# Four probability buffers, and the probability products of eight units issued together

## The chip, the core and the metric

The kernel runs on one core of a Trainium2 chip. The metric is the device time of one execution in microseconds (us). A core has five engines with queues of their own: TensorE (PE in the profile; PEld is its weight load), VectorE (DVE), ScalarE (ACT), GpSimd (POOL) and SyncE (SP, which issues the DMAs). They are ordered among each other only by semaphores.

## The reference

There are 8 batch rows of 512 tokens and 256 features. Each goes through a cross-attention with 16 heads of size 16 and then through a two-layer network without a nonlinearity, both with a normalisation ahead and a residual behind:

```python
qh = split_heads(layernorm(x) @ Wq.T + bq) / sqrt(16)
kh = split_heads(ctx @ Wk.T + bk)
vh = split_heads(ctx @ Wv.T + bv)
attn = softmax(einsum('bhqd,bhkd->bhqk', qh, kh), axis=-1)     # 512 x 512 for each head
y = x + einsum('bhqk,bhkd->bhqd', attn, vh) @ Wo.T + bo
h1 = layernorm(y) @ W1[b].T + b1[b]                            # 256 -> 1024, weights of its own for each b
out = y + h1 @ W2[b].T + b2[b]                                 # 1024 -> 256
```

## The kernel before

One batch row is one turn of a loop: `turns` writes out turns 0, 1, 6 and 7 and runs turns 2 to 5 as a hardware loop. A turn has 64 units, numbered u. The 16 heads form four quads of four heads. A unit is one head of a quad and one block of 128 keys, and four units that follow each other (a group, kc or n in the code, 16 groups in a turn) are the four heads of a quad for the same key block.

For each unit TensorE computes two score products:

- `st` (L449) gives the scores transposed, keys on the partitions, into one of two PSUM banks (`st0`, `st1`). ScalarE takes their exponential into a probability buffer (`exp`, L728).
- `nat` (L439) gives the scores of a unit 28 units ahead the other way round into one of three banks. VectorE takes their row maximum (L896), which is later subtracted inside `st`.

`st` and `nat` use 64 and 63 rows of the PE array, in the two halves of it, so that a `st` and a `nat` run side by side. `st(u)` waits until `exp(u-2)` has emptied its bank.

When the four exponentials of a group are there, `pv` (L463) multiplies the four heads' probabilities with their values. These four products use 32 columns of the array each and also run side by side. The trace shows eight matmul records for each `pv`: a first pass of four and a second pass of four. One `pv` fills one bank, `pv_bank`, over the four key blocks of a quad. ScalarE copies the sums out after groups 3 and 11 (`even_quad`, L756) and 7 and 15 (`odd_quad`, L768).

The order of TensorE's work is written out by hand. `turn` takes two units at a time (u0 = 0, 2, 4, ...): two `st` with their `nat`, at every second pair a `pv`, then the `jobs` of these two units. Jobs are all the rest, spread over the 64 units by tables: the values, keys and queries of the next row, the output projection of the previous row, its network (`w21_part`, L549, multiplies the two weight matrices together; `z` applies the product), transposes (L481), and the transpose of a quad's maxima (`maxT`, L495). Jobs have waits of their own. The one that matters below is at u = 39: the second half of the transposed `yT` overwrites bank `misc1`, and waits until ScalarE has copied the weight product out of it (`w21_copy_first`, L784, which stands behind `exp(38)` in ScalarE's order).

ScalarE too has a fixed order: the exponentials by unit, and between them by the unit's number its other work. After `exp(6)` and after `exp(7)` come two activations each that normalise the next row (L773). After `exp(22)` come the copy of the last quarter of the projections (L748) and the masking of the even quad's result (L761).

Probabilities have two buffers, `probs0` and `probs1`, group n in buffer n mod 2. `exp` of a group's first unit waits until the `pv` of two groups ago is done. `pv(n)` is issued after the `st` of units 4n+6 and 4n+7, four units behind the group's last: at u0 = 6, 10, 14, ..., 62 and at u0 = 2 of the next turn.

Of the kernel before, what the change touches and what calls it, by code (L numbers as in the profile page):

```python
# [30 lines left out]
ACT = mybir.ActivationFunctionType  # L31
AX = mybir.AxisListType

P = 128
B = 8
S = 512
# [8 lines left out]
UNITS = QUADS * 16  # L45
# [33 lines left out]
def xattn_ffn(nc, x, ctxT, wqT, bq, wkT, bk, wvT, bv, woT, bo, w1, b1, w2T, b2, out):  # L79
    with ExitStack() as stack:  # L80
        def sb(name, shape, dt=F32):
            return stack.enter_context(nc.sbuf_tensor(name, shape, dt))
# [4 lines left out]
        def sem(name):  # L87
            return stack.enter_context(nc.semaphore(name))
# [32 lines left out]
        vs = sb("vs", [P, C, H, 32])  # L121
        neg_max = sb("neg_max", [P, 2, 16])
        max_hi = sb("max_hi", [16, P], F32R)
        probs = [sb(f"probs{i}", [P, 4, S]) for i in range(2)]
        even_ctx = sb("even_ctx", [P, S])
        even_sum = sb("even_sum", [P, S])
        pair_ctx = sb("pair_ctx", [P, S])
# [48 lines left out]
        pv_done = sem("pv_done")  # L176
# [9 lines left out]
        exp_done = sem("exp_done")  # L186
# [59 lines left out]
        def st_of(u, prep):  # L246

            return (st_bank + nat_bank)[u % 3] if not prep and u >= LAST_ST else st_bank[u % 2]

        def nats_of(b, u, post, prep):  # L250

            if not post and FIRST_LEAD + 2 * u < u + LEAD:
                return [(b, FIRST_LEAD + 2 * u + i) for i in range(2)]
            n = u + LEAD
            if n < UNITS:
                return [(b, n)]
            return [(b + 1, n - UNITS)] if prep else []
# [4 lines left out]
        def wait(eng, s, value):  # L262

            if not (isinstance(value, int) and value <= 0):
                eng.wait_ge(s, value)
# [158 lines left out]
        def _(pe):  # L424
# [7 lines left out]
            def nat(b, n):  # L432
                g, c, (jj, jp) = n // 16, n % 16 // 4, NAT_HEADS[n % 4]
                rows = slice(HALF * jp, HALF * jp + KN)
                if n % 16 == 0:
                    wait(pe, stacked[g], STACKS * (b + 1))

                wait(pe, max_done, UNITS * b + {0: -3, 1: 0, 2: -1, UNITS - 1: n - 1}.get(n, n - 2))
                mm(nat_of(n)[:, :], qs[rows, 2 * g + jj, c * P:(c + 1) * P], ks[rows, 2 * g + jj, :],  # L439
                   start=True, stop=True).then_inc(nat_done, 1)  # L440

            def st(b, u, prep):
                g, kc, (jj, jp) = u // 16, u % 16 // 4, ST_HEADS[u % 4]
                rows = slice(HALF * jp, HALF * jp + KS)
                if u % 16 == 0:
                    wait(pe, max_rows, 16 * (4 * b + g + 1))

                wait(pe, exp_done, UNITS * b + u - (2 if not prep and u >= LAST_ST + 2 else 1))
                mm(st_of(u, prep)[:, :], ks[rows, 2 * g + jj, kc * P:(kc + 1) * P], qs[rows, 2 * g + jj, :],  # L449
                   start=True, stop=True).then_inc(st_done, 1)  # L450

            def pv(b, n):
                g, kc = n // 4, n % 4
                if kc == 0:
                    wait(pe, v_stacked, 4 * b + g + 1)
                    pair = 2 * b + g // 2
                    if g % 2:
                        wait(pe, even_out, pair + 1)
                    else:
                        wait(pe, odd_out, pair)  # L460
                wait(pe, exp_done, UNITS * b + 4 * n + 4)
                for j in range(4):
                    last = mm(pv_bank[32 * j:32 * j + 32, :], vs[:, kc, 4 * g + j, :],  # L463
                              probs[n % 2][:, j, :], start=(kc == 0), stop=(kc == 3),
                              tile_position=(0, 32 * j), skip_group_check=True)
                last.then_inc(pv_done, 1)

# [167 lines left out]
            def turn(b, post, prep, load):  # L635
                for u0 in range(0, UNITS, 2):
                    for u in (u0, u0 + 1):
                        st(b, u, prep)
                        for row, n in nats_of(b, u, post, prep):
                            nat(row, n)  # L640
                    if u0 % 4 == 2:
                        if u0 > 4:
                            pv(b, u0 // 4 - 1)
                        elif post:
                            pv(b - 1, 15)
                    for u in (u0, u0 + 1):
                        jobs(b, u, post, prep)

# [28 lines left out]
            pe.wait_ge(rows_set, 2)  # L677
            pe.wait_ge(ones_in, 16)
            turns(pe, turn)
            pv(LAST, 15)  # L680
            pe.wait_ge(last_comb, 1)
            pe.wait_ge(exp_done, UNITS * B)
# [39 lines left out]
        def _(act):  # L722
            def exp(b, u, prep):
                kc, j = u // 4, u % 4
                wait(act, st_done, UNITS * b + u + 1)
                if j == 0:
                    wait(act, pv_done, 16 * b + kc - 1)
                act.activation(probs[kc % 2][:, j, :], st_of(u, prep)[:, :], ACT.Exp).then_inc(exp_done, 1)  # L728

            def xT_copy(b, f, bank):  # L730
                wait(act, xT_done, 2 * b + f + 1)
# [73 lines left out]
            def turn(b, post, prep, load):  # L805
                for u in range(UNITS):
                    exp(b, u, prep)
                    if post:
                        if u == 0:
# [468 lines left out]
```

## Time and profile before

| | |
|---|---|
| device time, median of 3 runs | 616.38 us (615.13 to 617.4) |
| span of the profiled execution, first to last instruction | 613.0 us |
| TensorE busy | 584.0 us (95%) |
| VectorE busy | 458.9 us (75%) |
| ScalarE busy | 397.0 us (65%) |
| GpSimd busy | 221.2 us (36%) |
| mean granted TensorE clock | 0.989 |
| starts of turns 0 to 7, first `st` | 42.4, 106.9, 176.9, 247.5, 318.2, 388.9, 459.6, 529.5 us |

The profiled execution's own device time is not given apart from its span; the span is 3.4 us below the median of the runs. The turns in the middle are alike: each takes 70.7 us. The last turn takes 60 us up to its last products, because it prepares no next row. Matmuls are pipelined, so a record's duration is longer than the distance to the next start. How long TensorE is held by something is read here from the distance between starts.

### The profile page before, as it was taken

The page shows a single profiled execution, that of the slowest core. Times are in us where ns is not written, and L with a number is a line of the kernel's source. Part 1 is how long each engine was busy: PE and PEld are TensorE (multiplying, and loading weights), DVE is VectorE, ACT ScalarE, POOL GpSimd, SP SyncE. Part 2 cuts the span into 40 slices and gives each one's busy share as a digit, 9 for nine tenths or more (in the row PEclk, how much of TensorE's full clock was granted, in tenths as well). Part 3 has the DMA queues.
Part 4 walks back from the last instruction along what each step waited for, and adds up shares of the span by engine and source line. Part 5 has one row for each costly group of instructions (what it writes and reads, how often), then busy time and mean ns, then how long its engine had stood idle before and what let it go on. Part 6 is the DMA issues. An engine that isn't in the chain of part 4 may idle for free.

```text
span 613.0 us, 11485 instructions
## 1 busy us (share of the span) xinstructions
PE 584.0 (95%) x3380; PEld 296.0 (48%) x3380; DVE 458.9 (75%) x854; ACT 397.0 (65%) x746; POOL 221.2 (36%) x298
## 2 busy tenths in 40 slices
PE   7899989999999999999999999999999999889997
PEld 7545323545454544545444544445445454335457
DVE  5698787878888778787888777878788788786124
ACT  4217776776767586776667776676767766776741
POOL 5011028213660148212570138411481146313721
PEclk9969999999999999999999999999999999999999
DMA  8730333263224614254132823256042622260100
GB/s 291 186 93 2 86 90 105 54 215 115 81 62 131 213 40 140 54 194 133 45 95 55 264 61 117 47 161 189 8 137 53 208 54 76 66 208 2 69 21 34
DMA packets 34076, 65.23 MB, mean 106 GB/s; under 512 B 9778, under 2 KB 11642, under 8 KB 31994
## 3 DMA queue, kind: packets, MB, share of 16 engines
q1 hardware_dynamic: 34042, 64.81, 35.6%
q8 instruction: 17, 0.28, 0.2%
q14 instruction: 17, 0.14, 0.1%
HBM read 34.65 MB, written 4.44 MB: 64 GB/s over the span
## 4 chain that ended last, share of the span: by engine, by line
PE 83%; ACT 7%; issue 3%; POOL 2%; DVE 2%; DMA 1%; SPq 1%; ACTq 0%; DVEq 0%; POOLq 0%
PE st L449 20%; PE misc L471 20%; PE pv L463 18%; PE misc L549 11%; PE nat L439 8%; ACT probs L728 4%; PE misc L481 2%; ACT hi L748 1%; PE nat L430 1%; DMA bq_in<-bq 1%; PE misc L530 1%; ACT normedT_hi L741 1%; PE nat L471 1%; ACT normedT_hi L734 0%; POOL b_part L1185 0%
## 5 line engine op out<-in xcount | busy, mean ns | idle before, releaser
L896 DVE TENSOR_REDUCE neg_max<-nat 128x1 f32<-128x512 f32 x512 | 330.5, 679 | 78.9 <-PE nat L439 77.9
L728 ACT ACTIVATE probs<-st 128x512 f32<-128x512 f32 x505 | 283.3, 597 | 161.8 <-PE st L449 156.9
L449 PE MATMUL st<-qs,ks 64*128 64x512 f32 x505 | 200.9, 461 | 18.7 <-ACT probs L728 18.6
L439 PE MATMUL nat<-ks,qs 63*128 63x512 f32 x512 | 208.1, 471 | 1.9 <-DMA qs<-hi 1.1
L463 PE MATMUL pv<-probs,vs 128*32 128x512 f32 x1024 | 136.4, 605 | 0.0
L449 PEld LDWEIGHTS st<-qs,ks 64*128 64x128 f32 x505 | 80.5, 185 | 112.0 <-ACT probs L728 73.6
L439 PEld LDWEIGHTS nat<-ks,qs 63*128 63x128 f32 x512 | 83.4, 187 | 11.8 <-DVE neg_max L896 7.0
L549 PE MATMUL misc<-w_in 128*128 128x256 f32 x256 | 80.7, 411 | 0.0
L1147 POOL TENSOR_TENSOR pair_ctx<-pair_ctx,inv_sum 128x512 f32<-128x512 f32 x15 | 19.1, 1276 | 118.7 <-DMA inv_sum<-inv_dram 118.7
L549 PEld LDWEIGHTS misc<-w_in 128*128 128x128 f32 x256 | 40.6, 189 | 42.9 <-issue 35.5
L463 PEld LDWEIGHTS pv<-probs,vs 128*32 128x32 f32 x1024 | 20.1, 108 | 38.7 <-issue 35.8
L1123 POOL TENSOR_SCALAR var_eps<-mean_var 128x4 f32<-128x4 f32 x16 | 3.6, 226 | 97.3 <-DVE mean_var L913 96.8
L918 DVE SCALAR_TENSOR_TENSOR lo<-misc,bqk,hi 128x512 fp32r<-128x512 f32 x30 | 22.5, 751 | 14.9 <-ACT hi L748 14.9
L1139 POOL COPY vs<-v_nat 128x256 f32<-128x256 f32 x32 | 12.6, 398 | 56.5 <-PE pv L463 44.2
L1157 POOL TENSOR_TENSOR ctx_lo<-ctx_in,ctx_hi 128x1024 fp32r<-128x1024 f32 x7 | 16.7, 2381 | 44.8 <-ACT ctx_hi L797 44.8
L1152 POOL TENSOR_TENSOR attnT_lo<-pair_ctx,attnT_hi 128x512 fp32r<-128x512 f32 x15 | 19.1, 1275 | 32.8 <-ACT attnT_hi L803 32.8
L1170 POOL TENSOR_TENSOR y<-y,b_all 128x256 f32<-128x256 f32 x28 | 19.6, 732 | 19.9 <-ACT normed L773 19.9
L962 DVE SCALAR_TENSOR_TENSOR pair_ctx<-pv,half_hi,even_ctx 128x512 f32<-128x512 f32 x15 | 11.3, 751 | 18.6 <-ACT odd_sum L768 18.6
L1185 POOL TENSOR_TENSOR b_part<-b_part 128x256 f32<-128x256 f32 x32 | 23.4, 732 | 2.5
L1163 POOL TENSOR_TENSOR y<-y,bo_all 128x256 f32<-128x256 f32 x32 | 22.6, 736 | 0.0
L924 DVE TENSOR_TENSOR normedT_lo<-misc,normedT_hi 128x512 fp32r<-128x512 f32 x28 | 19.0, 680 | 3.7 <-ACT normedT_hi L741 3.7
L748 ACT ACTIVATE hi<-misc,bqk 128x512 fp32r<-128x512 f32 x30 | 20.5, 684 | 1.2 <-PE misc L471 1.0
(168 smaller groups left out, 803.5 us busy)
## 6 DMA issues: line engine op xcount, KB each, us to landing
w_in<-w SPq DMA_DIRECT2D x8, 1024.0 KB
w_in<-w2T SPq DMA_DIRECT2D x8, 1024.0 KB
ks<-hi SPq DMA_DIRECT2D x64, 128.0 KB, 2.4
qs<-hi SPq DMA_DIRECT2D x64, 128.0 KB, 2.5
x_in<-x SPq DMA_DIRECT2D x8, 512.0 KB, 3.4
ctx_in<-ctxT SPq DMA_DIRECT2D x8, 512.0 KB, 4.3
ks<-lo SPq DMA_DIRECT2D x32, 128.0 KB, 2.4
qs<-lo SPq DMA_DIRECT2D x32, 128.0 KB, 2.6
```

What stands on the lines that cost most here:

```text
L439: mm(nat_of(n)[:, :], qs[rows, 2 * g + jj, c * P:(c + 1) * P], ks[rows, 2 * g + jj, :], start=True, stop=True).then_inc(nat_done, 1)
L449: mm(st_of(u, prep)[:, :], ks[rows, 2 * g + jj, kc * P:(kc + 1) * P], qs[rows, 2 * g + jj, :], start=True, stop=True).then_inc(st_done, 1)
L463: last = mm(pv_bank[32 * j:32 * j + 32, :], vs[:, kc, 4 * g + j, :], probs[n % 2][:, j, :], start=(kc == 0), stop=(kc == 3), tile_position ...
L471: last = mm(dst, left[i], right[j], start=start and n == 0, stop=stop and n == 2)
L549: last = mm(misc[bank][:, 0:D], w1_in[:, o, f * P:(f + 1) * P], w2_in[:, o, :], start=(o == 0), stop=(o == OC - 1))
L728: act.activation(probs[kc % 2][:, j, :], st_of(u, prep)[:, :], ACT.Exp).then_inc(exp_done, 1)
L748: act.activation(hi[:, which, m, :], misc[bank][:, :], ACT.Identity, bias=bqk[:, which, m:m + 1]).then_inc(hi_ready, 1)
L896: dve.tensor_reduce(neg_max[:, g % 2, at:at + 1], nat_of(n)[:, :], AX.X, ALU.max, negate=True).then_inc(max_done, 1)
L918: dve.scalar_tensor_tensor(lo[:, which, m, :], misc[bank][:, :], bqk[:, which, m:m + 1], hi[:, which, m, :].bitcast(F32), ALU.add, ALU.sub ...
L1163: last = pool.tensor_tensor(y[:, c, :], y[:, c, :], bo_all[:, :], ALU.add)
L1170: last = pool.tensor_tensor(y[:, c, :], y[:, c, :], b2_all[:, :], ALU.add)
L1185: pool.tensor_tensor(b2_part[:, k, :], b2_part[:, k, :], b2_part[:, 4, :], ALU.add).then_inc(b2_step, 1)
```

## The change

Four probability buffers replace two. Group n is in buffer n mod 4, and the first `exp` of a group waits for the `pv` of four groups ago. On TensorE two `pv` are issued together at every fourth pair of units: at u0 = 10 groups 0 and 1, at 18 groups 2 and 3, and so on up to 58; at u0 = 2 of the next turn groups 14 and 15. The last turn issues group 14 alone at u0 = 62 and group 15 at the end, as before. So the groups with odd numbers stay where they were and those with even numbers come four units later. Nothing is computed otherwise.

```diff
-        probs = [sb(f"probs{i}", [P, 4, S]) for i in range(2)]
+        probs = [sb(f"probs{i}", [P, 4, S]) for i in range(4)]
...
                 wait(pe, exp_done, UNITS * b + 4 * n + 4)
                 for j in range(4):
                     last = mm(pv_bank[32 * j:32 * j + 32, :], vs[:, kc, 4 * g + j, :],
-                              probs[n % 2][:, j, :], start=(kc == 0), stop=(kc == 3),
+                              probs[n % 4][:, j, :], start=(kc == 0), stop=(kc == 3),
                               tile_position=(0, 32 * j), skip_group_check=True)
...
-                    if u0 % 4 == 2:
-                        if u0 > 4:
-                            pv(b, u0 // 4 - 1)
-                        elif post:
-                            pv(b - 1, 15)
+                    if u0 % 8 == 2:
+                        for kc in (0, 1):
+                            if u0 > 8:
+                                pv(b, u0 // 4 - 2 + kc)
+                            elif post:
+                                pv(b - 1, 14 + kc)
+                    if u0 == UNITS - 2 and not prep:
+                        pv(b, 14)
...
                 if j == 0:
-                    wait(act, pv_done, 16 * b + kc - 1)
-                act.activation(probs[kc % 2][:, j, :], st_of(u, prep)[:, :], ACT.Exp).then_inc(exp_done, 1)
+                    wait(act, pv_done, 16 * b + kc - 3)
+                act.activation(probs[kc % 4][:, j, :], st_of(u, prep)[:, :], ACT.Exp).then_inc(exp_done, 1)
```

TensorE's order in a turn, from the `st` of unit 7 to the first job behind unit 11, before (L471 are projections of the next row, `x4` four products side by side):

```order
L449 MATMUL st1<-qs,ks 128x512
L439 MATMUL nat2<-ks,qs 128x512
L463 MATMUL pv<-probs0,vs 32x512 x4
L495 MATMUL misc1<-ident,neg_max 16x128
L449 MATMUL st0<-qs,ks 128x512
...
L471 MATMUL misc0<-ctx_lo,w_hi 128x512
L449 MATMUL st0<-qs,ks 128x512
...
L439 MATMUL nat0<-ks,qs 128x512
L463 MATMUL pv<-probs1,vs 32x512 x4
L481 MATMUL misc1<-ident,normed 128x128 x4
```

The same place in the changed kernel:

```order
L449 MATMUL st1<-qs,ks 128x512
L439 MATMUL nat2<-ks,qs 128x512
L495 MATMUL misc1<-ident,neg_max 16x128
L449 MATMUL st0<-qs,ks 128x512
...
L471 MATMUL misc0<-ctx_lo,w_hi 128x512
L449 MATMUL st0<-qs,ks 128x512
...
L439 MATMUL nat0<-ks,qs 128x512
L463 MATMUL pv<-probs0,vs 32x512 x4
L463 MATMUL pv<-probs1,vs 32x512 x4
L481 MATMUL misc1<-ident,normed 128x128 x4
```

The product of `probs0` has left its place between the units 7 and 8 and stands ahead of that of `probs1`, behind unit 11.

TensorE's order around units 38 and 39 in turn 1, before (the L481 in `misc1` is the second `yT`):

```order
L449 MATMUL st1<-qs,ks 128x512
L439 MATMUL nat0<-ks,qs 128x512
L463 MATMUL pv<-probs0,vs 32x512 x4
L481 MATMUL misc1<-ident,normed 128x128 x4
L449 MATMUL st0<-qs,ks 128x512
```

And in the changed kernel:

```order
L449 MATMUL st1<-qs,ks 128x512
L439 MATMUL nat0<-ks,qs 128x512
L481 MATMUL misc1<-ident,normed 128x128 x4
L449 MATMUL st0<-qs,ks 128x512
L439 MATMUL nat1<-ks,qs 128x512
```

The transpose into `misc1` now follows the score products of unit 39 directly. On the other engines no instruction changes its place; only the buffers and the value that the first `exp` of a group waits for are others.

## Rows read from the trace of the kernel before

**Rows 1.** The page, busy time of TensorE; the costliest group of ScalarE.

```profile
PE 584.0 (95%) x3380; PEld 296.0 (48%) x3380; DVE 458.9 (75%) x854; ACT 397.0 (65%) x746; POOL 221.2 (36%) x298
...
L728 ACT ACTIVATE probs<-st 128x512 f32<-128x512 f32 x505 | 283.3, 597 | 161.8 <-PE st L449 156.9
```

**Rows 2.** Busy time by engine in stretches: turn 3 and turn 7.

```profile
247.50:318.20 70.70, 69.07 (x407) 34.28 (x406) 55.77 (x104) 49.30 (x93) 27.84 (x38) 1.00 0.38 113
...
529.50:589.80 60.30, 55.88 (x322) 24.41 (x322) 31.39 (x59) 43.71 (x84) 21.80 (x29) 1.00 0.23 76
```

**Rows 3.** Waits of TensorE: who for whom, us in total, times, longest.

```profile
PE st L449 <- ACT probs L728: 18.6, 46, 0.6
```

**Rows 4.** Timeline (start, duration, engine, line, work, idle before): one `pv`, its second pass.

```profile
308.66 1.06 PE L463 MATMUL pv<-probs,vs 128*32 128x512 f32 x8
...
309.12 0.61 PE L463 MATMUL pv<-probs,vs 128*32 128x512 f32 x4
...
309.66 0.28 PE L495 MATMUL misc<-ident,neg_max 128*16 128x128 f32 x1
```

**Rows 5.** Timeline, turn 3, units 6 to 9.

```profile
254.41 0.60 ACT L728 ACTIVATE probs<-st 128x512 f32<-128x512 f32 x1 [0.47 <-PE st L449]
254.79 1.06 PE L463 MATMUL pv<-probs,vs 128*32 128x512 f32 x8
254.90 1.08 ACT L773 ACTIVATE normed<-x_in,shift,rstd 128x256 f32<-128x256 f32 x2
255.88 0.58 ACT L728 ACTIVATE probs<-st 128x512 f32<-128x512 f32 x1
256.51 0.18 PEld L449 LDWEIGHTS st<-qs,ks 64*128 64x128 f32 x1 [0.33 <-ACT probs L728]
```

**Rows 6.** Timeline, turn 3, units 22 to 25.

```profile
273.11 0.60 ACT L728 ACTIVATE probs<-st 128x512 f32<-128x512 f32 x1
273.24 1.06 PE L463 MATMUL pv<-probs,vs 128*32 128x512 f32 x8
273.60 0.68 ACT L748 ACTIVATE hi<-misc,bqk 128x512 fp32r<-128x512 f32 x1
274.17 0.72 ACT L761 ACTIVATE even_ctx<-even_sum,half_lo 128x512 f32<-128x512 f32 x1
274.78 1.79 ACT L728 ACTIVATE probs<-st 128x512 f32<-128x512 f32 x3
275.43 0.50 PE L449 MATMUL st<-qs,ks 64*128 64x512 f32 x1 [0.49 <-ACT probs L728]
```

**Rows 7.** Timeline, turn 3, units 38 and 39.

```profile
292.42 1.06 PE L463 MATMUL pv<-probs,vs 128*32 128x512 f32 x8
292.78 0.38 ACT L784 ACTIVATE w_half<-misc 128x256 f32<-128x256 f32 x1
293.42 0.42 PEld L481 LDWEIGHTS misc<-ident,normed 128*128 128x128 f32 x4 [0.84 <-ACT w_half L784]
```

**Rows 8.** Timelines of ACT and PE, turn 3, units 14 to 17.

```profile
263.40 1.12 ACT L728 ACTIVATE probs<-st 128x512 f32<-128x512 f32 x2
...
263.60 1.06 PE L463 MATMUL pv<-probs,vs 128*32 128x512 f32 x8
...
265.50 0.50 PE L449 MATMUL st<-qs,ks 64*128 64x512 f32 x1
```

**Rows 9.** Timeline, end of turn 3: the `exp` of unit 55, the `st` of unit 57.

```profile
309.42 0.59 ACT L728 ACTIVATE probs<-st 128x512 f32<-128x512 f32 x1
...
310.64 0.39 PE L449 MATMUL st<-qs,ks 64*128 64x512 f32 x1
```

**Rows 10.** Timeline of PE, turn 7: `st` of units 14, 16 and 18.

```profile
541.27 0.49 PE L449 MATMUL st<-qs,ks 64*128 64x512 f32 x1 [0.45 <-ACT probs L728]
...
543.19 0.50 PE L449 MATMUL st<-qs,ks 64*128 64x512 f32 x1
...
544.37 0.50 PE L449 MATMUL st<-qs,ks 64*128 64x512 f32 x1 [0.45 <-ACT probs L728]
```

## The prediction, written before the changed kernel was run

> **What bounds the kernel now.** I read the page's busy times first: TensorE is busy 584.0 of 613.0 us, ScalarE 65% [rows 1]. By this alone every 0.1 us taken from TensorE's order is a gain. Then the stretches, turn by turn. Turn 3 stands for turns 1 to 6: TensorE 69.1 of 70.7 us, ScalarE 49.3 [rows 2]. So TensorE still waits 1.6 us a turn, and the list of waits says for whom: `st` for the exponentials, 18.6 us in 46 waits over the whole run [rows 3]. Few waits, but they tell that ScalarE is late at certain places although it is idle a third of the time. The reason is the coupling: `st` has two banks, so TensorE can run only two units ahead of ScalarE, and an `exp` follows its `st` by about half a us. ScalarE's spare time is worth nothing where its other work is bunched. So I went last through the timeline of one turn, and at each `pv` asked what TensorE would have done had the `pv` not been there. That is what the change does at every second one.
>
> **What is saved.** One `pv` holds TensorE from 308.66 to 309.66 us, 1.00 us: first pass 0.46, second 0.54 [rows 4]. The matmul durations overlap, so only the starts count. The second pass is 0.08 us longer; it is the one behind which the array goes over from four column tiles to another shape. Two `pv` in a row are four passes with one such end: three by 0.46 and one by 0.54, 1.92 us, instead of 2.00. No row shows two `pv` in a row on a free machine, so bounds: at the one end all four passes are like the first, 4 × 0.46 = 1.84; at the other the wait and the semaphore between the two hold them apart and the pair costs 2.00. I take 1.89, a little below 1.92, since the weights of the third pass can load behind the second pass as those of the second do behind the first. This is 0.11 us for a pair. There are 63 pairs (8 in each of 8 turns, less the last, whose groups 14 and 15 stay apart): 7 us at most.
>
> The Trainium skill (TensorEngine Tiling (Array Packing), Tiling Modes) says that changing the tiling mode drains TensorE, changing only the tile doesn't. The longer second pass agrees [rows 4]. By this rule alone, with everything else hidden, the change gives 613.0 − 7 = 606 us of span, a gain of 1.1%.
>
> **What is moved.** The odd groups stay; the even ones go four units later. So in each turn eight slots lose 1.00 us of TensorE work (u0 = 6, 14, 22, 30, 38, 46, 54, 62) and eight grow from 1.00 to 1.89 us (u0 = 2, 10, ..., 58), by 0.89 each. If a slot's 1.00 us comes back only in part, because TensorE runs into a wait that the `pv` had covered, the part is lost: the 0.89 is paid in any case four units on. What comes back, in turn 3:
>
> - u0 = 6: nothing. ScalarE works without a pause from `exp(6)` at 254.41 through two normalisations and `exp(7)` (255.88 to 256.46), and `st(9)` starts at 256.51, right behind, after a wait of its own [rows 5]. The chain starts from `st(6)`, ahead of the `pv`. Without the `pv` TensorE is at `st(9)` a us earlier and waits a us longer.
> - u0 = 14: 1.00. The exponentials of 14 and 15 end at 264.52, `st(16)` starts at 265.50 [rows 8], and `st(17)` right behind it. A us earlier, at 264.50, it just meets them.
> - u0 = 22: nothing. Behind `exp(22)` at 273.11 stand 0.68 and 0.72 us of other work; `exp(23)` is done at 275.38, and `st(25)` starts at 275.43 after a wait of 0.49 [rows 6]. This chain too starts ahead of the slot.
> - u0 = 30: 1.00, by the same comparison as at 14 on its own units.
> - u0 = 38: 0.26. The transpose behind the `pv` waits for `w21_copy_first`, which ends at 293.16. Today it starts at 293.42, with the `pv` (from 292.42) as cover [rows 7]. Without it, it could start at 292.42 and has to wait until 293.16.
> - u0 = 46: 1.00.
> - u0 = 54: about 0.8. `exp(55)` is behind the mask and ends at 310.01; `st(57)`, now at 310.64, can come only 0.6 earlier [rows 9]. Some 0.2 come back at `st(58)` and `st(59)`, which wait a little today.
> - u0 = 62: 0.97; the first two `st` of the next turn have about as much room as those of 16 and 17.
>
> Together 5.0 of 8.0 us. Paid: 8 × 0.89 = 7.1. The longer pause at u0 = 34 takes away a wait of some 0.1 us behind it. The larger waits after units 12 to 15 and 40 to 43 are not taken away: there ScalarE starts its chain from the delayed `st` and is late all the same. A middle turn: 7.1 − 5.0 − 0.1 = +2.0 us.
>
> **The two ends.** In turn 7 and in the second half of turn 0 long stretches have no jobs, and the two-bank loop sets the pace: two units with a `pv` take 1.92 us (541.27 to 543.19), without 1.18 (543.19 to 544.37) [rows 10]. There a slot gives back 0.74. Eight units take 2 × (1.92 + 1.18) = 6.20 now and 3 × 1.18 + 1.92 + 0.89 = 6.35 then. By the same ledger (estimates for their own slots, from the two kinds of slot above) turn 0 has 7 pairs (6.2 us paid) and gets back 0, 1.0, 0, 0.74, 0.7, 0.74, 0.5 and 1.0 = 4.7, and 0.4 of waits near its end: +1.1. Turn 7 pays 7.1 and gets back 0.8, 0.74, 0, 1.0, 0.25, 1.0 and 1.0 (u0 = 62 keeps its `pv`) = 4.8, and 0.6 of waits: +1.7.
>
> **What costs nothing.** The new waits for buffers: the first `exp` of group n waits for `pv(n-4)`, which is issued at the latest at u0 = 4n − 6, six units ahead. The copies out of `pv_bank` follow groups 3, 7, 11 and 15, which are odd and stay. The other four `pv` that start a quad get four units more to wait for the copy. VectorE and the DMA queue see the same order. VectorE is nearest to a wait at `nat` in units 7, 33 and 39, and TensorE's shift there is below what is left or is bounded by ScalarE already.
>
> **The sum.** 1.1 + 6 × 2.0 + 1.7 = 14.8 us. The span goes from 613.0 to 627.8, and the median, 3.4 us above the span today, from 616.4 to 631.
>
> **The rivals.**
> - *TensorE's order alone counts* (faster). Then all eight slots give back their full us and only the 0.11 a pair remain: 616.4 − 7 = 609.5. For it: TensorE busy 95%. Against it: the three chains above, where a wait stands in the trace already, right behind the slot. 0.08.
> - *The pair doesn't merge* (slower still). Each `pv` costs 1.00 as before; 63 × 0.11 = 7 us more: 638. For it: each `pv` has waits of its own in front, and no row shows how a second one starts. 0.12. It shows as a distance of 2.00 us over sixteen matmuls.
> - *ScalarE catches up in part.* If the chain at units 6 to 9 or 22 to 25 is less rigid (the pair ahead of it gives ScalarE a pause of 1.9 us), one of the two us comes back in each turn: 15 − 7 = +8, 624. For it: ScalarE idles 162 us before exponentials. Against it: both chains start from an `exp` that waited for its `st` or ends an idle queue, so nothing queued can be worked off earlier. 0.12.
> - The Trainium skill (TensorEngine Tiling (Array Packing), PSUM Bottleneck) warns that once TensorE is packed, the engines that empty PSUM become the bound. Here this is not so on average, ScalarE being busy 65%, but at the places above it is what decides; that is the forecast itself.
>
> **Chances.** Forecast 0.66, the rivals 0.08, 0.12 and 0.12; 0.02 is for anything else. No change, within 0.5% (3 us, about what a measurement of this kernel can tell), would need most of the lost slots to come back, and takes 0.06 out of the cases between; faster 0.08, slower 0.86. The range for 8 times in 10 is 618 to 640: below it lie the first rival and part of the third, above it a merged price with further waits.
>
> **What would show it.** Right: sixteen `pv` matmuls over 1.9 us; waits of `st` for `probs` up from 18.6 us to about 35 (2 us more in each turn); `st(9)` and `st(25)` of a turn as far behind `exp(6)` and `exp(22)` as now (2.10 and 2.32 us), with waits of over 1 us; the transpose of unit 39 waiting 0.7 us for L784; a middle turn of 72.7 us. Wrong: a middle turn at or below 70.7; waits for `probs` that stay at 19 us.

## The result, and the profile after

The changed kernel takes 648.24 us (647.75 to 649.21, 3 runs) against 616.38; the ratio is 1.049, with a 95% interval from 1.042 to 1.056. The direction of the forecast was right and its size was not: 631 was said, 640 was the upper end. A repetition beside the kernel before on one chip (the last experiment below) gave 648.09 us (647.55 to 650.50), 1.045 times the kernel before there (1.037 to 1.054). Medians are over all executions, while a ratio leaves out those over 1.5% above the fastest of their kernel, so that a ratio below can lie some tenths of a per cent off the quotient of the medians beside it.

| us | before | after |
|---|---|---|
| span of the profiled execution | 613.0 | 646.0 |
| TensorE busy | 584.0 | 597.6 |
| mean granted TensorE clock | 0.989 | 0.96 |
| turns 0 to 6 | 64.5, 69.9, 70.7, 70.7, 70.7, 70.7, 69.9 | 68.4, 73.7, 74.3, 75.9, 74.3, 75.9, 75.1 |
| turn 7 and the end | 83.5 | 86.0 |

The turns are differences of starts given to 0.1 us.

The device time of the profiled execution after is 647.75 us, 1.75 above its span.

TensorE's waits in the changed kernel (who for whom, us in total, times, longest), which answer to [rows 3]:

```profile
PE st L449 <- ACT probs L731: 32.8, 69, 1.2
PE misc L481 <- ACT w_half L787: 5.3, 7, 1.0
```

Both lines are close to the forecast: waits for the exponentials up from 18.6 to 32.8 us (about 35 was said), and a new one of 0.76 us on average in each of seven turns for the copy of the weight product (0.7 was said).

The pair, from PE's timeline (start, duration, engine, line, work, count), beside [rows 4]:

```profile
337.78 1.92 PE L463 MATMUL pv<-probs,vs 128*32 128x512 f32 x16
339.64 0.38 PE L471 MATMUL misc<-w_hi,ctx_hi 128*128 128x256 f32 x1
```

Sixteen matmuls hold TensorE for 339.64 − 337.78 = 1.86 us, a little less than the 1.89 of the forecast. So the merging works.

Units 6 to 9 of turn 4, beside [rows 5]:

```profile
342.62 0.60 ACT L731 ACTIVATE probs<-st 128x512 f32<-128x512 f32 x1 [0.41 <-PE st L449]
...
343.11 1.08 ACT L776 ACTIVATE normed<-x_in,shift,rstd 128x256 f32<-128x256 f32 x2
...
344.10 0.58 ACT L731 ACTIVATE probs<-st 128x512 f32<-128x512 f32 x1
344.73 0.49 PE L449 MATMUL st<-qs,ks 64*128 64x512 f32 x1 [0.89 <-ACT probs L731]
345.23 0.79 PE L471 MATMUL misc<-ctx_hi,w_hi 128*128 128x512 f32 x1
345.82 0.63 PE L471 MATMUL misc<-ctx_hi,w_lo 128*128 128x512 f32 x1
```

`st(9)` starts 2.11 us after `exp(6)` (344.73 − 342.62); it was 2.10. The `pv` is gone from between and nothing came of it. The wait is 0.89 us; over 1 us was said. What the forecast did not have is in the last two rows. The job behind it is the same as in the kernel before, but a product of it (`ctx_hi,w_lo`) takes 0.63 us instead of 0.40, as here in turn 3 of the kernel before:

```profile
257.36 0.40 PE L471 MATMUL misc<-ctx_hi,w_lo 128*128 128x512 f32 x1
```

The stretches of the changed kernel say why (length, busy time of PE, PEld, DVE, ACT, POOL, then the granted clock):

```profile
340.00:345.20 5.20, 4.31 (x25) 2.61 (x23) 4.62 (x8) 4.12 (x9) 0.30 (x1) 1.00 0.32 71
345.20:348.60 3.40, 3.40 (x10) 2.32 (x10) 1.10 (x3) 1.42 (x3) 0.00 (x0) 0.50 0.57 130
348.60:352.00 3.40, 3.40 (x28) 1.14 (x24) 2.31 (x5) 1.72 (x4) 0.00 (x0) 1.00 0.00 0
```

From 345.2 to 348.6 us the granted clock is 0.50, 1.2 instead of 2.4 GHz. It gets 10 matmuls done in a time in which 28 are done behind it (of other shapes, with the pair among them). Ahead of the fall TensorE had stood still for 0.89 us. The page's row of the clock shows the rest:

```profile
PEclk9958899989998999898998999988998999999999
```

Of each such 16 us slice, one stretch of 3.4 us at half clock leaves a tenth less. There are 11 of them after the start, called falls of the clock from here on. Each begins at most 1.4 us behind the start of a `st(9)` or a `st(25)` ahead of which TensorE had been idle for 0.88 to 1.17 us. There are 14 such waits, one at each of the two units in turns 0 to 6; three of them have no fall behind them. The turns 2 to 5 run the same instructions, and yet the wait of 1.10 us at `st(25)` is followed by a fall in the turns 3 and 5 and not in 2 and 4. What decides between them is not shown. The kernel before has no fall between its start and its end; its longest wait of `st` is 0.6 [rows 3].

The waits of units 22 to 25 (turn 4), beside [rows 6]:

```profile
363.46 0.60 ACT L731 ACTIVATE probs<-st 128x512 f32<-128x512 f32 x1
...
365.78 0.50 PE L449 MATMUL st<-qs,ks 64*128 64x512 f32 x1 [1.09 <-ACT probs L731]
```

`st(25)` starts 2.32 us after `exp(22)` (365.78 − 363.46), as before and as said, behind a wait of 1.09 us.

And the transpose of unit 39, beside [rows 7]:

```profile
383.89 0.38 ACT L787 ACTIVATE w_half<-misc 128x256 f32<-128x256 f32 x1
...
384.32 0.66 PE L481 MATMUL misc<-ident,normed 128*128 128x128 f32 x4 [0.72 <-ACT w_half L787]
```

### The profile page after: what moved, and what is told of

Same layout as the page of the kernel before. It is cut to its first block, busy times and chain, and to the rows that moved or that the text cites. A ratio compares the mean times of both kernels' runs of the same rounds, so it can differ in the third digit from the quotient of the medians.

```text
span 646.0 us, 11483 instructions
## 1 busy us (share of the span) xinstructions
PE 597.6 (93%) x3380; PEld 316.2 (49%) x3380; DVE 459.4 (71%) x854; ACT 398.6 (62%) x746; POOL 221.4 (34%) x298
## 4 chain that ended last, share of the span: by engine, by line
PE 80%; ACT 11%; issue 4%; DVE 2%; DMA 1%; ACTq 1%; SPq 1%; DVEq 0%
PE misc L471 19%; PE st L449 19%; PE pv L463 19%; PE misc L549 10%; PE nat L439 7%; ACT probs L731 5%; PE misc L481 2%; ACT hi L751 1%; ACT even_ctx L764 1%; ACT normed L776 1%; PE nat L430 1%; PE misc L530 1%; DMA bq_in<-bq 1%; ACT normedT_hi L744 1%; ACTq L265 1%
## 5 line engine op out<-in xcount | busy, mean ns | idle before, releaser
L449 PE MATMUL st<-qs,ks 64*128 64x512 f32 x505 | 205.7, 471 | 32.9 <-ACT probs L731 32.8
L439 PE MATMUL nat<-ks,qs 63*128 63x512 f32 x512 | 215.0, 482 | 2.1 <-DMA qs<-hi 1.2
L449 PEld LDWEIGHTS st<-qs,ks 64*128 64x128 f32 x505 | 83.3, 189 | 127.5 <-ACT probs L731 75.6
L463 PE MATMUL pv<-probs,vs 128*32 128x512 f32 x1024 | 125.7, 608 | 0.0
L439 PEld LDWEIGHTS nat<-ks,qs 63*128 63x128 f32 x512 | 86.9, 192 | 12.8 <-DVE neg_max L899 7.0
L463 PEld LDWEIGHTS pv<-probs,vs 128*32 128x32 f32 x1024 | 26.9, 111 | 61.2 <-issue 48.5
L776 ACT ACTIVATE normed<-y,shift,rstd 128x256 f32<-128x256 f32 x29 | 15.8, 591 | 12.5 <-POOL shift L1135 12.5
L481 PE MATMUL misc<-ident,normed 128*128 128x128 f32 x112 | 18.0, 283 | 5.3 <-ACT w_half L787 5.3
```

Of the source, the lines that this page charges most:

```text
L481: last = nc.tensor.transpose(misc[bank][:, c * P:(c + 1) * P], normed[:, c, f * P:(f + 1) * P], ident[:, :])
L776: act.activation(normed[:, c, :], src[:, c, :], ACT.Identity, bias=shift[which][:, c:c + 1], scale=rstd[which][:, c:c + 1]).then_inc(norm_ ...
```

## What the 33 us are made of

The span grew by 646.0 − 613.0 = 33 us, the median by 32. Two kinds of turn can be told apart. In the profile of the repetition, turn 2 has no fall of the clock, so that it shows the ledger alone, that is what the slots give back and what the pairs cost; in the first profile, turn 3 has two falls:

```profile
183.10:255.90 72.80, 68.55 (x407) 35.57 (x406) 55.98 (x105) 49.43 (x94) 27.69 (x38) 1.00 0.38 111
```

```profile
258.80:334.70 75.90, 71.65 (x409) 37.45 (x408) 56.12 (x105) 49.51 (x94) 27.91 (x38) 0.96 0.36 105
```

A middle turn without a fall takes 72.8 us, +2.1 over 70.7 [rows 2]; +2.0 was forecast. A fall adds 1.5 to 1.6 us ((75.9 − 72.8) / 2, and 74.3 − 72.8 in a turn with one). 11 × 1.55 = 17 us, and 33 − 17 = 16 us are left for the ledger, which said 14.8. The profile of the repetition has almost the same span, 645.9 us, with seven falls behind the 14 waits and three stretches' worth of half clock in turn 7.

## The experiments

The experiments ran on three chips, each beside the kernel before on the same chip, and the ratios are to that. There the kernel before scatters by up to 10 us from run to run (615 to 625 us), and so do some of the variants. Its slower runs were not traced. In two of the traced variants, "Pairs only where the slot is free" and "Thinning ScalarE's chains", the clock stood at 0.50 for 27 to 31 us of the first 57 us, and turn 0 began 6 to 7 us late; this is a likely reason, not a shown one, for the others. So I read single turns beside the medians.

**The buffers alone.** All groups alone at their old places (the diff gives the edit in effect):

```diff
                     if u0 % 8 == 2:
-                        for kc in (0, 1):
+                        for kc in (1,):
...
-                    if u0 == UNITS - 2 and not prep:
-                        pv(b, 14)
+                    if u0 % 8 == 6:
+                        pv(b, u0 // 4 - 1)
```

> Four probability buffers and the wait for the pv of four groups ago, but every pv alone at its old place (u0 = 6, 10, 14, ...). Theory (the moved pv uncover waits of TensorE, and its clock falls behind the longest of them): the buffers cost nothing, 616 us within 2 us, granted clock 0.99 as before, no stretch at half clock after the start. Rival (the buffers themselves, by their place in SBUF or by the changed wait, cost the time): well above, 630 to 648.

Measured: 618.9 us beside 621.1, ratio 0.999 (0.994 to 1.004). Turn 3 takes 70.70 us, and the profiled run, 615.57 us at a clock of 0.989, has no fall after the start. The buffers cost nothing.

**Pairs only where the slot is free.**

```diff
-                        for kc in (0, 1):
+                        for kc in (0, 1) if u0 in (2, 18, 34, 50) else (1,):
...
-                    if u0 == UNITS - 2 and not prep:
-                        pv(b, 14)
+                    if u0 % 8 == 6 and ((u0 + 4) % UNITS not in (2, 18, 34, 50) or u0 == UNITS - 2 and not prep):
+                        pv(b, u0 // 4 - 1)
```

> Changed kernel, but only the pairs at u0 = 2, 18, 34, 50 (their partners come from the slots 62, 14, 30, 46, behind which TensorE has no wait near); the other groups alone at their old places. 31 pairs. Theory: each pair takes 1.86 instead of 2.00 us, 31 x 0.14 = 4.3 us less, hardly any new wait, no stretch at half clock: 612 us, between 611 and 615. Rival (pairing as such slows the kernel or the clock): half of the whole change, about 632.

Measured: 619.0 us beside 621.1, ratio 1.000 (0.995 to 1.006). Neither number was met: the pairs do no harm, but they gain nothing. Turn 3:

```profile
254.10:324.90 70.80, 69.01 (x409) 35.20 (x408) 55.83 (x105) 49.40 (x94) 28.01 (x37) 1.00 0.38 113
```

The 4 × 0.14 us are eaten by small waits where the forecast had none. One has its row: the job of unit 15 waits for VectorE as soon as it comes a us earlier (PE's timeline of turn 3):

```profile
271.45 0.50 PE L471 MATMUL misc<-ctx_hi,w_hi 128*128 128x512 f32 x1 [0.15 <-DVE normedT_lo L927]
```

By the starts of `st` beside those of the kernel before, slot 14 gives back 0.8 us instead of 1.0, 0.2 us more is lost in the first units of a turn (slot 62), and the pair at u0 = 34 costs 0.1 more than the others. Together this is the whole gain.

**Pairs only where the slot covered a wait.** The same edit with (10, 26, 42, 58).

> Changed kernel, but only the pairs at u0 = 10, 26, 42, 58 (their partners come from the slots 6, 22, 38, 54, which covered a wait). 32 pairs. Theory: paid 4 x 0.86 = 3.4 us a turn, given back 0 + 0 + 0.3 + 0.8 = 1.1, so 2.3 us a turn and 19 us in all, and the falls of the clock stay (11 by 1.7 us = 19 us): 654 us, between 646 and 660, more than the whole change. Rival (pairing as such): 632.

Measured: 648.2 us beside 621.1, ratio 1.048 (1.039 to 1.058), no less than the whole change with half its pairs. That is inside the range; the profiled run (643.6 us) has five falls behind the 14 waits at `st(9)` and `st(25)` and two in turn 7, where 11 falls were said. A turn without a fall:

```profile
181.20:254.30 73.10, 68.86 (x407) 34.86 (x406) 55.85 (x104) 49.34 (x93) 27.69 (x38) 1.00 0.39 110
```

+2.4 us a turn, where 2.3 was said. Against the kernel before, `st(8)` starts 0.9 us earlier in this turn, `st(9)` at the same time, `st(12)` 0.8 later; `st(24)` 0.1, `st(25)` 0.8, `st(28)` 1.6; `st(38)` 1.6, `st(40)` 1.4, `st(44)` 2.3. That is the ledger slot by slot. All the damage outside the clock comes from these four slots.

**Filling the waits.** The changed kernel, with matmuls in the two long waits whose results nobody needs:

```diff
                             nat(row, n)
+                        if u == 8 and prep:
+                            wait(pe, odd_out, 2 * b)
+                            stay_warm(4, 7)
+                        if u == 24:
+                            wait(pe, even_out, 2 * b + 1)
+                            stay_warm(5, 7)
```

> Changed kernel, with matmuls added that only fill TensorE's wait between st(8) and st(9) (4 of 128 columns, turns 0 to 6) and between st(24) and st(25) (5, all turns), written to the free pv bank. Theory (the clock falls because TensorE stands still there): the filler takes 1.1 and 1.3 us, about the waits of 1.0 and 1.25 us, so no stretch at half clock and the ledger alone is left: 616 + 15 = 631 us, between 629 and 636. Rival (the clock falls for another reason, such as the column-tiled pairs): the clock stays at 0.96 and the time at 648 or a little above.

Measured: 639.7 us beside 621.1, ratio 1.033 (1.024 to 1.042). Better than the changed kernel by 8 us, with work added, but above the 636 expected. In the profile no stretch at half clock is left behind `st(9)` or `st(25)`; the waits for exponentials are down to 18.1 us, none over 0.6. Turn 3 takes 73.0 us at full clock, 0.2 more than a turn of the changed kernel without a fall. Three falls are left, at 450.7, 590.7 and 614.5 us: two behind the units 42 and 43, where TensorE waits 0.3 to 0.5 us, one in the end part. In the profiled run (637.8 us) they, the fillers' 0.2 us a turn beyond the waits, and the ledger make the rest. The fillers were expected to win all 17 us of the falls and won 8: the falls at their places are gone, some others came.

**The waits without the pairs.** Every `pv` alone; two of them behind the waits they had covered (changed from "The buffers alone"):

```diff
-                    if u0 % 8 == 6:
-                        pv(b, u0 // 4 - 1)
+                    if u0 % 8 == 6 and u0 not in (6, 22):
+                        pv(b, u0 // 4 - 1)
+                    if u0 in (8, 24):
+                        pv(b, u0 // 4 - 2)
```

> Four buffers, every pv alone and at its old place but two: groups 0 and 4 are issued behind the st of units 8, 9 and 24, 25 instead of ahead of them. No two pv stand together. Theory (the wait that a moved pv uncovers is what stops the clock): each of the two slots gives back nothing and the pv is paid behind it, 2.0 us a turn, 15 us in all, and TensorE's waits at st(9) and st(25) are as long as in the changed kernel (about 0.9 and 1.2 us), so that the clock falls as often, about 11 times by 1.5 us: 645 us, between 636 and 652, granted clock near 0.96. Rival (the clock falls because two pv stand together): clock 0.99 and 631 us.

Measured: 636.9 us (633.9 to 648.9) beside 621.3, ratio 1.029 (1.018 to 1.041); the time is in the range, near its low end. A turn without a fall takes 72.7 us, +2.0 as expected. The profiled run has three falls, two of them behind one of these waits and the third behind a wait of 0.6 us at `st(25)` of turn 7, and there is no pair in this kernel. One is at 354.9 us (a wait, a single `pv`; then the stretch at half clock):

```profile
354.90 0.50 PE L449 MATMUL st<-qs,ks 64*128 64x512 f32 x1 [1.10 <-ACT probs L733]
...
355.41 1.94 PE L463 MATMUL pv<-probs,vs 128*32 128x512 f32 x8
```

```profile
355.50:358.90 3.40, 3.40 (x15) 1.74 (x16) 1.02 (x3) 0.54 (x1) 0.00 (x0) 0.51 0.36 104
```

So a pair is not needed for a fall; falls come behind the wait without one. But 14 waits as long as in the changed kernel brought 2 falls here and 11 there. The kernels with the pairs at these waits vary as well: 7 of 14 in the repetition, 5 of 14 in "Pairs only where the slot covered a wait". The granted clock of the four runs here is 0.981, 0.978, 0.971 and 0.955, while the changed kernel's seven runs stay at 0.955 to 0.960. Whether the order around the wait makes a fall likelier was not settled.

**Thinning ScalarE's chains.** The changed kernel with

```diff
-                        if u == 6:
+                        if u == 5:
...
-                        if u in (6, 7):
-                            normalise(0, b + 1, x_in, 2 * (u - 6), 2 * (u - 6) + 2)
+                        if u in (5, 6, 7, 8):
+                            normalise(0, b + 1, x_in, u - 5, u - 4)
...
-                    if u in (22, 54):
+                    if u in (26, 58):
                         mask_even(b, u // 32)
```

> Changed kernel with ScalarE's work thinned at two places: the four normalising activations behind exp(5), (6), (7), (8), one each, instead of two behind exp(6) and two behind exp(7); the mask behind exp(26) and (58) instead of (22) and (54). Theory (rigid ScalarE chains keep the slots from giving back): st(9) comes 0.5 us earlier, st(25) 0.6, st(57) and its neighbours 0.2: 1.3 us a turn, 10 us in all; and with the waits halved the clock falls hardly ever, up to 16 us more: 622 us, between 618 and 630, clock 0.98 to 0.99. Rival (the clock does not follow the waits): 638 at a clock of 0.96.

Measured: 631.9 us beside 621.3, ratio 1.019 (1.010 to 1.028), 16 us better than the changed kernel, and 2 us above the upper end expected. The waits at `st(9)` and `st(25)` are halved in turns 1 to 6, to 0.4 to 0.6 us. Turn 3:

```profile
258.90:330.50 71.60, 68.61 (x409) 35.70 (x408) 55.78 (x105) 49.30 (x94) 28.04 (x38) 1.00 0.39 111
```

71.6 us is 1.2 below 72.8, where 1.3 was said. Turns 1 to 6 are free of falls. The profiled run (635.2 us, the slowest of the four) still has two in turn 0 and two in turn 7, one of them twice as long, and 6 us more at the start; these are what it is above the sum.

**And the copy of the weight product earlier.** As above, with `w21_copy_first(b)` behind `exp(37)` instead of `exp(38)`.

> As e5_spread, and the copy of the weight product out of bank misc1 behind exp(37) instead of exp(38). Theory: the transpose of unit 39 no longer waits 0.75 us in the seven turns that have it: 5 us less than e5_spread, 617 us. Rival (that wait is covered by something else): as e5_spread.

Measured: 619.8 us beside 621.3, ratio 0.999 (0.994 to 1.005). The transpose's wait is gone from the list, and turn 3 takes 70.7 us, the time of before:

```profile
250.50:321.20 70.70, 68.72 (x407) 35.90 (x406) 55.63 (x105) 49.18 (x94) 27.99 (x38) 1.00 0.39 113
```

The step is 0.9 us a turn, near the wait of 0.76. The medians differ by more, 12 us where 5 was said; between the two profiled runs the rest is the late start and the falls in turn 7, which this one does not have. With three pieces of ScalarE's work moved, the kernel with pairs is as fast as the kernel before. Whether pairing costs nothing any more is another question, which the next experiment answers.

**Thinning alone.** The kernel before, two buffers and single `pv`, with the edit of "Thinning ScalarE's chains".

> The kernel before, two buffers and single pv, with ScalarE's work thinned as in e5_spread. Theory: TensorE's waits of 0.2 us at st(9) and 0.65 us at st(25) go, 0.7 us a turn: 5 us less than the kernel before. Rival (covered elsewhere): the same as before.

Measured: 609.6 us beside 621.3, ratio 0.984 (0.974 to 0.994), the fastest kernel of the study. Turn 3 takes 69.7 us instead of 70.7, and TensorE waits 14.7 us for exponentials instead of 18.6:

```profile
245.20:314.90 69.70, 68.58 (x407) 34.13 (x406) 55.67 (x104) 49.37 (x93) 27.95 (x38) 1.00 0.38 114
```

The gain is 0.4 us at `st(9)` and 0.6 at `st(25)`; 0.7 in all was expected. Part of the 1.6% is the scatter of the kernel before: beside its runs with the same granted clock (0.986 to 0.989, 615.0 to 617.5 us) the three runs at 608.5 to 609.7 us are 6 to 7 us faster, about 1%, which is what 1.0 us a turn says.

The turn of "And the copy of the weight product earlier", with its pairs, stands 1.0 us above this one. Against the thinned kernel without pairs, the slots 6 and 22 still give back next to nothing, by the starts of `st`: thinning brought `st(9)` and `st(25)` forward in both kernels. So pairing still costs a us a turn, and the work moved on ScalarE pays for it.

**Both.** Thinned, the copy earlier, and pairs at the free slots only.

> The best of both by the ledger: four buffers, pairs only at u0 = 2, 18, 34, 50, ScalarE's work thinned as in e5_spread, the copy of the weight product behind exp(37). In e2_free_slots these pairs came to nothing in a middle turn (0.5 us saved, 0.5 lost at the slots 62 and 14 and at u0 = 34), and e7_before_spread gained 1.0 us a turn by the thinning alone. Theory: the same as e7_before_spread within 2 us, 608 to 611 us, clock 0.986 to 0.989. Rival (merging adds to it once ScalarE is out of the way): 605.

Measured: 612.6 us beside 621.1, ratio 0.987 (0.979 to 0.995); turn 3 takes 69.8 us. That is as the theory said for the turn, and the pairs at the free slots add nothing. The time is 1.6 us above the upper end of 611: the profiled run has a clock of 0.98 and a fall each in turns 0 and 7.

**The changed kernel again.**

> The changed kernel once more, beside the kernel before on one chip, to see how steady the falls of the clock are from run to run. Theory: each run has 9 to 13 stretches at half clock behind the two waits, clock 0.95 to 0.96, 645 to 650 us. Rival (the first runs fell by chance in a bad phase): runs near 632 at 0.98 are among them.

Measured: 648.09 us, granted clock 0.955 to 0.960 in the four runs, and no run near 632. The one that was profiled has seven falls behind the 14 long waits, where 9 to 13 were said, and two later ones in turn 7, one of them twice as long, behind waits of 0.3 to 0.6 us. So the time is steady, and the places of the falls are not.

## Why the prediction was right or wrong

- *The saving.* Right. A pair takes 1.86 us, 0.14 less than two single `pv`.
- *What the slots give back.* Right, slot by slot. In the turn without a fall (by the starts of `st` beside turn 3 of the kernel before), 6 and 22 give back nothing, 14, 30 and 46 about 1.0, 38 0.2 (said: 0.26), 54 0.8 (said: about 0.8), 62 0.8 (said: 0.97), because the first units of the next turn lose 0.2. The pairs cost 0.86 each beyond a single `pv`, not 0.89, and the 0.1 us of waits that the pair at u0 = 34 was to take away did not come. Small errors cancel: a middle turn costs 2.1 us, where 2.0 was said.
- *The two ends.* Turn 0 has two falls and is 3.9 us longer; without them (3.1) 0.8 is left. In the repetition it has one fall and is 3.1 us longer, which leaves 1.5. 1.1 was said, between the two. Turn 7 with the end is 2.5 us longer without a fall; 1.7 was said.
- *What costs nothing.* Right: four buffers cost nothing ("The buffers alone"), and VectorE holds up TensorE no more than before (0.6 us in `nat`, both times).
- *The price of a wait.* Here the prediction failed. The step "TensorE is at `st(9)` a us earlier and waits a us longer" priced a wait at its length. The profile showed the clock at 0.989 and no fall in the whole middle, and the sum put the clock at nothing without giving a reason. Waits of TensorE of 0.88 to 1.17 us are followed, in 11 of 14 cases in the first profile, by 3.4 us at half clock, 1.55 us each: 17 us that the sum had not, half of the loss. With the waits filled the falls go from these places; with a wait and no pair they come too, though fewer; with the waits halved by another order on ScalarE they stay away from the middle turns. Why one such wait is followed by a fall and the next is not stays open.
- *The rivals.* "TensorE's order alone counts" fell with the first profile. "The pair doesn't merge" would have given 638 by a mechanism that isn't there: 1.86 us, not 2.00. "ScalarE catches up in part" did not happen: `st(9)` and `st(25)` stand as far behind `exp(6)` and `exp(22)` as before. None of them had the clock.

The Trainium skill (TensorE: Matmul & The Clock Gate, HAM oscillation) warns of idle gaps of TensorE that bring the clock down, in kernels that wait for DMAs much longer than a us. The direction agrees with this trace; the size does not: here waits of about one us between dense work already came before a fall.

## What to carry to other kernels

An instruction of the busiest engine that stands ahead of a wait may be free where it stands. Before moving it, ask at each place what the engine would have waited for without it; the answer is in the distance between the neighbour's last release and the next start, and here it foretold each slot of a middle turn to 0.2 us.

A wait of TensorE can cost more than its length: a kernel that runs at full clock throughout can lose it by a change that turns short waits into waits of about a us. The sum should have a term for that with wide bounds: here a fall followed 2 to 11 of 14 such waits, at 1.5 us each. When TensorE waits in a few places for an engine that is idle a third of the time, first spread that engine's own work: moving the normalisation and the mask gained 1.0 us of a turn of 70.7, and merging matmuls nothing.

## What was not expected of the hardware

- The granted clock falls to 0.50 for 3.4 us behind waits of TensorE of 0.88 to 1.18 us, 1.5 to 1.6 us lost each time, in 11 of 14 waits in one profile, 7 in the repetition, 5 with half the pairs and 2 where no two `pv` stand together. Single falls also came behind waits of 0.3 to 0.75 us, in turns 0, 5 or 7 of nine of the ten experiments' profiles, that of the repetition included. In the profile of the kernel before, whose longest wait of `st` is 0.6 us, and in that with four buffers alone there was none after the start.
- Sixteen column-tiled matmuls in four passes hold TensorE for 1.86 us, eight in two for 1.00: the two passes more cost 0.86.
